# The first key/value context goes to another buffer and the loads of batch 1 are issued ahead of batch 0, in a cross-attention kernel

## The reference, cut to what matters

```python
B, S, H, HEADS, C, T = 16, 100, 640, 8, 384, 4       # 722 context rows: 718 keys and 4 "ca" rows
query = x @ Wq                                        # [16, 100, 640]
keyt, valt = enc @ Wk, enc @ Wv                       # enc: the 718 context rows of each batch
hs = mha(query, keyt, valt)                           # 8 heads of 80, softmax over 718 keys
ca_q1 = einsum('btc,th->bch', ca, Wq_ca)[:, indices]
ca_hs1 = mha(ca_q1, x, x)                             # 100 x 100 for each head
ca_hs2 = mha(ca_hs1 @ Wq, ca @ Wk_ca, ca @ Wv_ca)     # softmax over 4
out = (hs + ca_hs2) @ Wout + b_out + x
```

## Time and profile before

| | us |
|---|---|
| median of 3 runs | 1004.24 |
| lowest and highest | 1001.93, 1004.46 |
| the profiled execution: its own time | 1004.24 |
| the profiled execution: its span | 1002.5 |
| PE busy | 985.5 (98%) |
| DVE busy | 652.0 |
| ACT busy | 490.8 |
| POOL busy | 342.9 |
| granted TensorE clock, mean over the span | 0.992 |

### The profile page before, as it was taken

The page is one execution under the profiler, slowest core; times in us unless marked ns, Lnnn a source line. Parts: engine busy times, 40 slices in busy tenths (PEclk is TensorE's granted clock), DMA queues, the critical chain, the costliest instruction groups (busy, mean ns, idle before and its releaser), DMA issues.

```text
span 1002.5 us, 20727 instructions
## 1 busy us (share of the span) xinstructions
PE 985.5 (98%) x6740; PEld 964.2 (96%) x6740; DVE 652.0 (65%) x1129; ACT 490.8 (49%) x895; POOL 342.9 (34%) x286
## 2 busy tenths in 40 slices
PE   9989999999999999999999999999999999998998
PEld 8989889999999999999999999999999999997997
DVE  6544676667667766667676767676766666667444
ACT  7524555555554546464636364636464545446110
POOL 5212253434252516161515243333333333416000
PEclk9979999999999999999999999999999999999999
DMA  7959978797879797979797979788887878795354
GB/s 264 307 192 257 266 190 210 166 202 168 191 172 195 171 187 177 187 181 185 181 182 185 181 184 181 191 171 202 170 201 162 210 162 193 171 213 152 98 181 146
DMA packets 154169, 190.12 MB, mean 190 GB/s; under 512 B 80928, under 2 KB 108192, under 8 KB 154144
## 3 DMA queue, kind: packets, MB, share of 16 engines
q1 hardware_dynamic: 147456, 177.44, 75.6%
q10 hardware_dynamic: 6688, 12.35, 3.7%
HBM read 81.56 MB, written 19.95 MB: 101 GB/s over the span
## 4 chain that ended last, share of the span: by engine, by line
PE 85%; DVE 5%; SPq 4%; DMA 3%; ACT 2%; issue 1%; ACTq 0%; DVEq 0%
PE psS L744 21%; PE psB L779 20%; PE psB L784 10%; PE psS L719 7%; PE psT L760 6%; PE psS L888 6%; PE psT L806 4%; PE psT L812 2%; SPq L382 2%; DMA encT_raw<-in_encT_dram 1%; PE psB L861 1%; SPq L379 1%; PE psB L838 1%; PE psT L813 1%; PE psS L944 1%
## 5 line engine op out<-in xcount | busy, mean ns | idle before, releaser
L744 PE MATMUL psS<-encT_keep,Wk_keep 128*128 128x360 f32 x1440 | 253.7, 329 | 0.0
L744 PEld LDWEIGHTS psS<-encT_keep,Wk_keep 128*128 128x128 f32 x1440 | 237.3, 188 | 0.9 <-issue 0.2
L779 PE MATMUL psB<-PT_h,encN_h 120*128 120x400 f32 x576 | 202.3, 351 | 0.0
L779 PE MATMUL psB<-PT_l,encN_h 120*128 120x400 f32 x576 | 198.8, 345 | 0.0
L1130 ACT ACTIVATE probs<-psS,negmax 100x718 f32<-100x718 f32 x128 | 110.2, 861 | 129.2 <-DVE negmax L1522 129.0
L606 POOL TENSOR_TENSOR encT_keep<-encT_raw,encT_keep 128x718 fp32r<-128x718 f32 x45 | 79.7, 1771 | 181.6 <-ACT encT_keep L1159 179.3
L1546 DVE TENSOR_TENSOR kT<-psS,kT 128x718 fp32r<-128x718 f32 x80 | 72.4, 905 | 94.9 <-ACT kT L1154 94.7
L614 POOL TENSOR_TENSOR encN_l<-enc_raw,encN_h 120x768 fp32r<-120x768 f32 x48 | 92.6, 1930 | 91.4 <-ACT encN_h L1166 90.0
L597 POOL TENSOR_TENSOR Mbd<-Mbd,fmask 128x320 fp32r<-128x320 f32 x48 | 45.8, 954 | 226.7 <-DMA Mbd<-m_split 224.1
L784 PE MATMUL psB<-PT_h,encN_l 120*128 120x400 f32 x576 | 120.4, 344 | 0.7 <-POOL encN_l L614 0.7
L1154 ACT ACTIVATE kT<-psS 128x718 fp32r<-128x718 f32 x80 | 61.7, 771 | 115.2 <-PE psS L744 110.0
(11 more groups left out here) (245 smaller groups left out, 1643.5 us busy)
## 6 DMA issues: line engine op xcount, KB each, us to landing
kstack<-kT SPq DMA_DIRECT2D x64, 448.8 KB
kstack<-kT SPq DMA_DIRECT2D x192, 112.2 KB
enc_raw<-in_encN_dram SPq DMA_DIRECT2D x48, 360.0 KB, 5.6
encT_raw<-in_encT_dram SPq DMA_DIRECT2D x45, 359.0 KB, 6.4
kstack<-kT SPq DMA_DIRECT2D x32, 359.0 KB
kstack<-kT SPq DMA_DIRECT2D x32, 269.2 KB
kstack<-kT SPq DMA_DIRECT2D x32, 179.5 KB, 3.6
kstack<-kT SPq DMA_DIRECT2D x64, 89.8 KB, 3.5
```

Of the source, the lines that this page charges most:

```text
L744: mm = pe.matmul(keys_in(f, first)[:, half, 0:HALF], w[:, c, f * 128:(f + 1) * 128], e[:, c, k0:k0 + HALF], start=(j == 0), stop=(j == 3 * ...
L779: pe.matmul(psB[:, 1, 0:RH], eN[0][:, k, cc], PT[p][:, k, rows], start=(k == 0 and p == 0), stop=False)
```

## The change

All of it lies in the first 150 us, in stage 1 and batch 0.

- encT[0] is loaded into `P_keep` and no longer into `encT_raw`. The buffer is the one of the WqT heads, so the DMA waits for hlo at 8 and stands behind `load_heads(6, 2)` and `load_q(0)` in SP's order.
- `enc0_high` and `enc0_low` come after head 6, head 7 and the query block (1, 4) on ACT and DVE; they stood before head 6.
- M is computed by whole heads: 0 after `query(1, 0)`, 1 and 2 after `query(1, 1)`, then 3, 4, 5, and 6 and 7 after `query(1, 5)`.
- The loads for batch 1 (`load_encT(1, 0..2)`, `load_ga(1)`) and the row layout of batch 0 (`load_enc(0, 0..2)`) are issued in one run ahead of batch 0, behind `lift(0, 2, heads=(3,))` and ahead of `lift(0, 2, heads=(4,))`. SP no longer waits for enc0lo.
- On ACT in batch 0, `k_high(0, 3)` comes ahead of the last stores of group 2, and `expo(0, 5)` comes behind `q_high(3, 5)`, `enc_high(0, 0)` and `store_q3(5)`.

```diff
-        enc0_raw = rawT
+        enc0_raw = P_keep[:, 0:CT * KEYS].rearrange("p (c k) -> p c k", c=CT)
...
                 load_ga(0, first=True)
-                sp.wait_ge(s["wlo"], 5)
-                sp.dma_start(enc0_raw, encT[0].rearrange("(c p) k -> p c k", p=128)).then_inc(s["encin"], 16)
                 sp.wait_ge(s["hlo"], 6)
                 load_heads(6, 2)
                 sp.wait_ge(s["v2st"], 32)
                 load_q(0, first=True)
+                sp.wait_ge(s["hlo"], HEADS)
+                sp.dma_start(enc0_raw, encT[0].rearrange("(c p) k -> p c k", p=128)).then_inc(s["encin"], 16)
                 store_q(1, 0, 3)
...
                 lift(0, 2, heads=(3,), first=True)
-                sp.wait_ge(s["enc0lo"], CT)
+                sp.wait_ge(s["wlo"], 5)
+                for c in range(CT):
+                    load_encT(1, c, first=True)
+                for c in range(PARTS):
+                    wait_apart(sp, s["xTlo2"], 3 * FT, s["passed_sp"])
+                    load_enc(0, c, first=True)
+                load_ga(1)
...
# SP's batch(i): load_encT(i + 1, c), load_enc(i, c) and load_ga(i + 1) only where i is not the first
...
-                def m_parts(n0, n1):
+                def m_head(h):
+
+                    pe.wait_ge(s["hlo"], h + 1)
+                    if h == 0:
+                        pe.wait_ge(s["k2lo"], 2)
+                        pe.wait_ge(s["v2lo"], 2)
+                        pe.wait_ge(s["qlo"], FT)
+                    for c in range(FT):
+                        for n, (w, k) in enumerate(products(wqT[h % WRING], k2T)):
...
-                parts = (0, 7, 14, 21, 28, 34, 40)
-                for j in range(NP):
+                for j, heads in enumerate(((0,), (1, 2), (3,), (4,), (5,), (6, 7))):
                     query(1, j)
-                    m_parts(parts[j], parts[j + 1])
+                    for h in heads:
+                        m_head(h)
...
# ACT, batch(i)
-                    if first:
-                        store_q2(4, FT)
-                        store_g2()
-                    else:
-                        u_high(i - 1, 2)
-                    k_high(i, 3)
-                    if first:
+                    if not first:
+                        u_high(i - 1, 2)
+                    k_high(i, 3)
+                    if first:
+                        store_q2(4, FT)
+                        store_g2()
                         q_high(3, 0)
...
                     xm_copy(i)
-                    expo(i, 5)
                     if first:
                         q_high(3, 5)
                         enc_high(i, 0, first)
                         store_q3(5)
+                    expo(i, 5)
                     xm_high(i)
...
# ACT, stage 1 (DVE the same with enc0_low, head_low, q_low)
                 q_high(1, 2)
-                for c in range(CT):
-                    enc0_high(c)
                 head_high(6)
                 q_high(1, 3)
                 head_high(7)
                 q_high(1, 4)
+                for c in range(CT):
+                    enc0_high(c)
                 q_high(1, FT)
```

More of the change, by code:

```diff
@@ L486, in batch @@
                         load_enc(i, 0)
-                    else:
-                        load_encT(i + 1, 0, first)
+                    elif not first:
+                        load_encT(i + 1, 0)
                     lift(i, 2, heads=(4,))
@@ L491, in batch @@
                         load_enc(i, 1)
-                    else:
-                        load_encT(i + 1, 1, first)
+                    elif not first:
+                        load_encT(i + 1, 1)
                     if not first:
@@ L500, in batch @@
                         load_wo(0)
-                    else:
-                        load_encT(i + 1, 2, first)
-                        if first:
-                            wait_apart(sp, s["xTlo2"], 3 * FT, s["passed_sp"])
-                        load_enc(i, 0, first)
+                    elif not first:
+                        load_encT(i + 1, 2)
+                        load_enc(i, 0)
                     lift(i, 4)
@@ L509, in batch @@
                         load_wo(1)
-                    else:
-                        load_enc(i, 1, first)
-                        load_enc(i, 2, first)
+                    elif not first:
+                        load_enc(i, 1)
+                        load_enc(i, 2)
+                    if not last and not first:
                         load_ga(i + 1)
+                    if not last:
                         load_x(i + 1)
@@ L984, in ca_values @@
                         mm.then_inc(s["v2"], 1)
-                def m_parts(n0, n1):
[L988 to L996, removed]
+                def m_head(h):
[6 more added lines that the diff above has]
+                        for n, (w, k) in enumerate(products(wqT[h % WRING], k2T)):
                             mm = pe.matmul(ps_m(c)[:, h * B * T:(h + 1) * B * T], w[:, c * 128:(c + 1) * 128],
-                                           k2[:, h, :], start=(k == 0), stop=(k == 2))
-                        if c == FT - 1:
-                            mm.then_inc(s["m"], 1)
+                                           k[:, h, :], start=(n == 0), stop=(n == 2))
+                    mm.then_inc(s["m"], 1)
                 def batch(i, first=False, last=False):
@@ L1805, in _ @@
                 q_low(1, 2)
-                for c in range(CT):
-                    enc0_low(c)
                 head_low(6)
@@ L1811, in _ @@
                 q_low(1, 4)
+                for c in range(CT):
+                    enc0_low(c)
                 q_low(1, FT)
```

## The result

| | median us | lowest, highest | ratio to before, 95% interval |
|---|---|---|---|
| before, in the runs beside the changed kernel | 1001.93 | 998.10, 1007.32 | |
| changed | 1010.62 | 1004.90, 1015.10 | 1.0067 [1.0045, 1.0091] |

The change makes the kernel 0.67% slower, some 6.7 us. By the prediction's own line of 0.3% the likeliest case was no change, and slower had a chance of 0.26. Its sum (1004.9) and range (up to 1009) were too low: 1.0067 of 1004.24 is 1011.0. One execution of the changed kernel took 2957.42 us; it counts in the median alone. The ratio is taken over more executions than the medians, and the text goes by it. The profiled execution of the changed kernel took 1004.10 us (span 1002.4), less than any of its timed ones, so its profile alone would say "no change".

The account below looks back on a forecast made before the run. PE, busy 98% of the span, was taken as the bound, so only its arrival at batch 1 could move. 1004.24 - 3.9 (stage 1) + 3.4 (loads) + 1.2 (exponential) = 1004.9, say 1005.0 us; range 1000 to 1009.

Parts of the forecast that it names:

- the prediction's own line of 0.3%: Whole kernel: 0.3%, 3 us, taken as about what a measurement can tell; it separates faster, same and slower.
- the likeliest case: Whole kernel: same, chance 0.52, against faster 0.22 and slower 0.26.
- Stage 1: the wait for head 6 goes: Stage 1: PE's 3.1 us wait for head 6 low parts disappears, with hlo 8 at 51.9 us.
- Against `keys(0, 0)` at 69.26 PE gains: Stage 1: PE ready at 63.3, less 2.1 us for the clock, gains 3.9 us, bounds 2.4 to 5.2.
- the wait for the stores: Stage 1: k_high(0, 0) waits for the stores of M; if the clock stays up, gain 6.0 on PE, about 5 on copies.
- rival (d): Stage 1: no gain, encT[0] only another late transfer, landing at 62; total 1008.8 us, chance 0.08.
- Rival (c): Stage 1: clock after the new wait stays down 13.8 us, losing 6.8 instead of 2.1; total 1009.7 us, chance 0.08.
- encT[0] is late next: Stage 1: encT[0] lands at 58.0, PE waits 3.5 us before keys(0, 0), then 4.3 us at half clock lose 2.1.
- Batch 0, the moved loads: Batch 0: head 4's lift lands 8.0 us later, k_high(0, 4) 4.7 late, turn(0, 2) 4.4; net loss 3.4 us.
- Batch 0, the moved exponential: Batch 0: keys(1, 0) starts 2.6 us late behind expo(0, 5); net loss 1.2 us, bounds 0 and 2.6.
- the P2x wait: Batch 0: PE's 1.1 us wait behind the DVE chain disappears, giving back 1.1 us and some tenths.
- some 2 us: Batch 0: a second clock fall, named as what would make the prediction wrong, not in the sum.

Follow-up runs that it names:

- before_again: The kernel before, unchanged, run once more for a second profile: 1001.45 us, 0.9988 of before.
- b_moved: The kernel before with only the loads of batch 1 and of the row layout moved ahead of batch 0: 1005.72 us, 1.0021 of before.
- after_again: The changed kernel, unchanged, run once more for a second profile: 1010.12 us, 1.0068 of before.
- a_fill: The changed kernel with 16 matmuls of 360 columns on PE ahead of keys(1, 0), results overwritten: 1006.10 us, 1.0037 of before.
- a_spread: The changed kernel with the loads of batch 1 and of the row layout spread between the lifts again: 1006.07 us, 1.0036 of before.
- a_stage1: The kernel before with only encT[0] in P_keep, its load and splits behind the heads: 1001.02 us, 0.9994 of before.
- b_expo5: The kernel before with only expo(0, 5) moved behind q_high(3, 5), enc_high(0, 0) and store_q3(5): 1003.87 us, 1.0014 of before.

## Why the prediction was right or wrong, step by step

The waits of batch 0 came as forecast. The time was too low by some 6 us, and two terms account for nearly all of it: the gain of stage 1 was put at 3.9 us and was 0.8, and the clock in batch 0 was put at nothing and cost 2.6.

PE's way to batch 1 can be cut at `keys(0, 3)`, where the lifts of batch 0 begin to matter, and at `keys(1, 3)`, behind all that the change touches. Of the 14 profiles, by which edits they have:

| | profiles | at `keys(0, 3)` | from there to `keys(1, 3)` | of it PE idle | mean clock in it |
|---|---|---|---|---|---|
| neither batch 0 edit | 6 | | 57.7 to 59.5, mean 58.5 | 3.6 | 1.00 |
| exponential moved | 2 | | 58.6, 61.6 | 4.5, 5.4 | 1.00, 0.97 |
| loads moved | 2 | | 63.0, 62.6 | 6.6, 6.0 | 0.97, 0.97 |
| both | 3 | | 63.7, 67.5, 66.0, mean 65.7 | 8.2 | 0.97, 0.92, 0.95 |
| both, filler before `keys(1, 0)` | 1 | | 61.4 | 4.0 | 1.00 |
| old stage 1 | 7 | 86.6 to 94.0, mean 90.1 | | | |
| new stage 1 | 7 | 88.3 to 90.5, mean 89.3 | | | |

Each is a window from the start of the one to the start of the other; idle is its length less PE's busy time. For four of them:

```profile
86.57:146.10 59.53, 55.13 (x341) 51.60 (x341) 41.53 (x71) 30.69 (x56) 20.72 (x15) 1.00 0.90 231
```

```profile
90.64:153.60 62.96, 56.32 (x342) 52.88 (x342) 41.74 (x71) 30.80 (x56) 20.31 (x15) 0.97 0.81 216
```

```profile
89.86:157.34 67.48, 58.55 (x341) 55.50 (x341) 38.47 (x71) 31.14 (x57) 20.39 (x15) 0.92 0.78 206
```

```profile
89.18:150.56 61.38, 57.36 (x358) 54.42 (x358) 38.06 (x69) 31.14 (x57) 20.82 (x15) 1.00 0.83 222
```

They are of before_again, b_moved, after_again and a_fill. PE's own work is the same 341 or 342 matmul records in all but the last, so busy time beyond the 54.9 us of the first group is the low clock, to within some tenths. Behind `keys(1, 3)` the span ends 849 to 858 us later, with no order between the groups: these 8 us, which the change doesn't touch, are one reason why a single execution says so little.

**"Stage 1: the wait for head 6 goes": the size failed, and it is the largest error.** The wait went, and the heads, encT[0] and M came as forecast or about one us earlier (low parts of encT[0] done at 60.4, forecast 61.5; two of M at 62.1, forecast 63.3). The failed step is "Against `keys(0, 0)` at 69.26 PE gains": 69.26 is the latest of seven profiles with the old stage 1, whose mean is 65.5 (62.8 to 69.3), because the 13.8 us of half clock were that execution's alone. The wait for head 6 itself stood in four of the seven (2.2 to 3.5 us, `keys(0, 0)` at 64.6 to 69.3); in the other three the clock had been low earlier or a filler stood there, PE came late, and it was gone (62.8 to 64.1).

The seven with the new stage 1 have 62.2 to 64.2, mean 63.0. What remained, 2.5 us, was mostly given back: `k_high(0, 0)` waits for the stores of M, and ran at 68.10 in the changed kernel, 5.9 us behind `keys(0, 0)`, and at 66.12 in the second profile of before, 3.3 behind. Between the means of seven it ran only 0.9 us earlier. The lift of block 0 and `k_high(0, 2)` come behind it, and PE, still 2.0 us ahead at `keys(0, 2)`, waited for them ahead of the first scores in six of the seven (0.8 to 2.1 us).

I had named the wait for the stores and priced it at one us, and only for a clock that stays up; the one at the first scores I had missed. At `keys(0, 3)` the gain is 0.8 us between means. The runs of stage 1 alone agree: -0.06% with 0.23% of uncertainty. My rival (d), no gain at all, has nearly the right number for another reason, which is luck: its late transfer didn't occur. Rival (c) didn't come true either: no low stretch behind 60 us was longer than 6.8 us with the new stage 1.

**"encT[0] is late next", the wait of 3.5 us and a clock fall: in part.** Of the seven, two had a wait of 2.2 to 2.6 us for the low parts of M, the others at most 0.4: PE itself was late, since its clock had fallen earlier, for 6.8 us in all, in a_spread for 10.2. Around one of the two waits the clock fell (for 6.8 us, a_stage1), around the other it didn't. In the changed kernel 6.7 us at 0.50 came before 44, where I had costed PE's way at the full clock.

**Batch 0, the moved loads: right in mechanism and nearly in size.** `k_high(0, 4)` ran 13.9 to 16.0 us behind `keys(0, 3)` with spread loads and 17.4 to 19.8 with moved ones, 3.7 late between means, forecast 4.7. `turn(0, 2)` came 17.0 to 19.1 behind it with spread loads and 20.4 to 22.8 with moved ones, 3.4 late between means, forecast 4.4. PE's idle time rose by 2.7 us (6.3 against 3.6), forecast 3.4.

That the sizes came out so near is in part luck, since two errors cancel. SP's run of loads took 7.2 us in the changed kernel, of which 6.4 are extra ahead of this lift, forecast 10.0. The last DMA of the lift was issued 12.1 us behind `keys(0, 3)` on the mean of the six profiles with moved loads, 6.8 on that of the eight others: 5.3 later, forecast 8.0. But I had it land in 3.5 us in either order. With moved loads it landed 5.8 to 7.2 us after its issue (in the changed kernel 5.9: issued by 100.76, landed just ahead of `k_high(0, 4)` at 106.76), without them 2.8 to 5.3, by the semaphore events of the traces: 2.3 longer between means, forecast nothing.

The Trainium skill, "DMA: Bandwidth & Descriptors", "Queues, rings and completion order", has a queue's descriptors consumed in ring order; the longer landing behind 1.8 MB of loads agrees with it, though it is less than the 6.4 us of the estimate, and no run here shows the order of the descriptors itself.

**Batch 0, the moved exponential: right but for the clock.** The wait of 2.8 us was in all five profiles of kernels with this edit and no filler, forecast 2.6; the P2x wait went in each, and in the two with spread loads idle time rose by 0.9 and 1.8, forecast 1.2. In one of these two the clock fell behind it as well.

**`k_high(0, 3)` and M by heads at nothing:** no run shows a cost. The first was not run by itself.

**The term that was missing: the clock in batch 0.** With both edits PE's idle time rose by 4.6 us (8.2 against 3.6), and 3.4 + 1.2 = 4.6 was forecast (that the tenth agrees is luck: the three profiles have 7.5, 8.9 and 8.2). But its busy time rose too, by 2.6 us (57.5 against 54.9): the clock fell for 3.4 us in the first profile, and twice in each of the other two. I named it, as what would make me wrong, with "some 2 us", and left it out of the sum without a reason, though the earlier trace rows had shown a fall right behind a wait of 3.1 us and the sum created waits of 4.4 and 2.6. With the measured terms the sum is 4.6 + 2.6 - 0.8 = 6.4 us, against 6.7 by the ratio. By ratios, taking back the loads gives 0.32%, the exponential 0.28%; that the parts add up to the 0.68% is not shown, with intervals of 0.3%. On the old stage 1 they don't seem to: alone they cost 0.21 and 0.14%, both together, with `k_high(0, 3)`, 0.97%. The surplus of 0.6% has an uncertainty of about 0.5, and whether it is the second clock fall, `k_high(0, 3)` or chance stays open.

## What to carry to other kernels

A single profile is one draw: before a gain is computed against "PE arrives at 69.26", ask whether the delay ahead of it is the kernel's or a clock fall of that execution, and what the next wait would be without it. Here a PE wait of 2 to 4 us cost its own length and, in 14 of 16 cases, up to half of a stretch at the lower clock behind it, mostly of 3 to 7 us, so a change that makes PE wait in two places may cost four terms and not two. Loads that nobody needs soon cost when they go ahead of small transfers that a copy waits for: here five loads of 360 KB and six small ones ahead of a lift had it issued 5.3 us later and land 2.3 us more slowly, and a copy with 4 us of slack came 3.7 us late.

## What the runs showed of the hardware

- The clock fell with no wait near, in a place that differed from execution to execution of one program: from 32 to 39 us in one profile of before, and there not at all in the other; from 37.3 to 44.0 in the changed kernel. Each time PE had just done narrow matmuls of 64 columns, and most of what it did next, at half clock, were the wide ones of a query. These low stretches lasted 3.4 to 7 us, against 13.8 in the first profile of before.
- Between 50 and 140 us the 14 profiles have 16 waits of PE from 2.1 to 4.1 us. In 14 the clock fell during the wait or within two us of its end, in two it did not (2.20 in after_again, 2.82 in b_expo5). Of the 34 waits from 0.9 to 1.9 us in the same stretch none had a fall so near.
- DVE's subtraction of a head's low part took 2.13 us with POOL at work in the earlier trace rows, and 0.94 and 1.17 in the changed kernel, where POOL ran as well: so POOL's presence alone doesn't set it. POOL's instruction beside the 2.13 was not one of those in the earlier trace rows, which end at 52.10, but a multiplication of 128x800 from 52.18 to 54.25; beside the 0.94 and 1.17 it subtracted 128x400. Beside such subtractions the last two low parts of encT[0] took 1.75 and 1.73 in the first profile of before, and 0.90 each without POOL in the changed kernel.
